# A decoder layer on one core: softmax sums on four column groups, their inverse copied to the other rows, values projected in the banks of q and k

## The reference, cut to what matters

```python
q = einsum('bse,hed->bhsd', x, Wq) + bq          # k and v alike
scores = einsum('bhsd,bhtd->bhst', q, k) / sqrt(64)
attn = softmax(where(causal, scores, -inf))
out = einsum('bhst,bhtd->bhsd', attn, v)
x = layernorm(x + out @ Wo + bo)
x = layernorm(x + cross_attention(x, ctx))
x = layernorm(x + fp8_ffn(x))
```

## Time and profile before

| what | us |
|---|---|
| median of 3 runs | 430.06 (429.84 to 430.45) |
| the profiled execution, whole | 428.27 |
| its span, from the first to the last instruction | 426.5 |
| PE busy | 385.7 |
| DVE busy | 307.5 |
| ACT busy | 237.6 |
| POOL busy | 239.8 |

### The profile page before, as it was taken

One profiled execution on the slowest core, in us unless ns is written; L12 is line 12 of the kernel. 1 busy time (PEld: TensorE's weight loads), 2 busy tenths in 40 slices (PEclk: granted clock), 3 DMA queues, 4 the chain that ended last, 5 costly groups with the idle time before them and its releaser, 6 DMA issues.

```text
span 426.5 us, 9900 instructions
## 1 busy us (share of the span) xinstructions
PE 385.7 (90%) x3698; PEld 274.1 (64%) x3698; DVE 307.5 (72%) x924; ACT 237.6 (56%) x352; POOL 239.8 (56%) x338
## 2 busy tenths in 40 slices
PE   3779999999999999999999999799999999998821
PEld 1567666776767776677766767577787776544410
DVE  0646887877887777887788877976535655689897
ACT  2335665556665566665666556464512155788941
POOL 3466876556665565655667556465824430231775
PEclk9989999999999999999999999999999999999985
DMA  8012011000000300000000000000000000000001
GB/s 259 12 6 54 3 15 27 4 8 5 5 1 5 100 2 2 3 4 1 2 3 2 2 2 3 0 2 2 3 1 2 2 0 2 2 2 2 25 26 51
DMA packets 41568, 6.96 MB, mean 16 GB/s; under 512 B 38320, under 2 KB 40240, under 8 KB 41392
## 3 DMA queue, kind: packets, MB, share of 16 engines
q1 hardware_dynamic: 41520, 6.32, 9.3%
HBM read 5.12 MB, written 1.05 MB: 14 GB/s over the span
## 4 chain that ended last, share of the span: by engine, by line
PE 64%; DVE 14%; ACT 7%; DMA 7%; issue 4%; SPq 3%; POOLq 0%; POOL 0%; DVEq 0%; ACTq 0%
PE banks L172 11%; PE banks L146 10%; PE banks L214 8%; PE banks L699 7%; DMA shift<-neg_max 6%; PE banks L152 4%; PE banks L191 4%; DVE unused L352 3%; PE banks L130 3%; PE banks L743 3%; PE banks L165 3%; SPq L523 3%; PE banks L756 3%; ACT q_hi L305 2%; PE banks L163 2%
## 5 line engine op out<-in xcount | busy, mean ns | idle before, releaser
L286 ACT ACTIVATE probs<-banks 128x768 f32<-128x768 f32 (+1 forms) x96 | 84.9, 884 | 114.1 <-PE banks L152 114.1
L352 DVE CUSTOM_DVE_ANT_0 unused<-banks,neg_mask 128x512 bf16<-128x512 f32 (+3 forms) x256 | 112.6, 487 | 38.8 <-PE banks L130 38.8
L451 POOL TENSOR_SCALAR_AFFINE_SELECT probs<-probs 128x256 f32<-128x256 f32 x128 | 51.2, 412 | 112.7 <-ACT probs L286 111.3
L172 PE MATMUL banks<-probs,v_nat 128*64 128x256 f32 (+3 forms) x512 | 74.4, 433 | 0.0
L172 PEld LDWEIGHTS banks<-probs,v_nat 128*64 128x64 f32 x512 | 36.6, 137 | 45.3 <-issue 40.5
L152 PE MATMUL banks<-shift,ones_r 64*128 64x256 f32 (+3 forms) x256 | 42.9, 329 | 6.7 <-DMA shift<-neg_max 6.6
L898 POOL TENSOR_TENSOR rstd<-var_e,halves 128x4 f32<-128x4 f32 (+1 forms) x16 | 14.4, 898 | 60.1 <-DVE var_e L974 59.8
L146 PE MATMUL banks<-q_hi,k_hi 64*128 64x256 f32 (+3 forms) x256 | 43.5, 334 | 1.7 <-ACT probs L286 1.7
L361 DVE SCALAR_TENSOR_TENSOR q_lo<-banks,bias_qk,q_hi 128x512 fp32r<-128x512 f32 x32 | 24.0, 751 | 25.8 <-ACT q_hi L305 25.8
L146 PE MATMUL banks<-q_hi,k_lo 64*128 64x256 f32 (+3 forms) x256 | 41.9, 321 | 0.0
L146 PE MATMUL banks<-q_lo,k_hi 64*128 64x256 f32 (+3 forms) x256 | 41.8, 320 | 0.0
(11 more groups left out here) (125 smaller groups left out, 826.1 us busy)
## 6 DMA issues: line engine op xcount, KB each, us to landing
shift<-neg_max SPq DMA_DIRECT2D x256, 0.5 KB, 2.0
attn_t<-w_qkv SPq DMA_DIRECT2D x1, 1344.0 KB, 7.0
attn_t<-xT SPq DMA_DIRECT2D x4, 256.0 KB, 7.2
x_s<-x_nat SPq DMA_DIRECT2D x1, 1024.0 KB, 5.1
wo_s<-wo SPq DMA_DIRECT2D x1, 512.0 KB, 3.9
out<-y_out SPq DMA_DIRECT2D x2, 256.0 KB, 3.1
out<-y_out SPq DMA_DIRECT2D x4, 128.0 KB, 1.7
neg_mask<-causal SPq DMA_DIRECT2D x1, 256.0 KB, 3.8
```

The costliest lines, as they stand in the source:

```text
L172: last = mm(o_ps[HALF[h], j * T:S], v_nat[:, v // 2 % 2, j, v % 2, HALF[h]], p_of(v, j, h, 0, S - j * T), start=(j == 0), stop=(j == NT - 1))
L286: nc.scalar.activation(probs[:, v % 2, AT[j]:AT[j] + 2 * n].rearrange("p (h s) -> p h s", h=2), st[:, :, 0:n], ACT.Exp, scale=D ** -0.5).t ...
L352: last = V.tensor_tensor_reduce(out=unused[:, h, at:at + n], in0=mx[:, h, at:at + n], in1=neg_mask[:, S - n:S], scale=-1.0, scalar=3.0e38, ...
L451: return nc.gpsimd.affine_select(out=blk, in_=blk, compare_op=ALU.is_ge, fill=0.0, base=0, pattern=pattern + [[1, T]], channel_multiplier=-1)
```

## The change

`sums` uses four column groups of 32 rows, one product each for two parts of the columns of either head. The first 32 rows of a head's 64 hold the sums of columns 0 to 255, the second 32 rows those of columns 256 to 511; the other half of every row is filled with 1.0 once, at the start. After `inverse`, the missing halves of `r_neg` are copied from one group of rows to the other: `spread` on ScalarE copies two pieces of 32 rows by 256 columns for head 0, and `inverse` on VectorE two for head 1. `normalise` waits for both, and stands one slot later, between the maxima and `q_lo`. Since bank 7 must keep its 1.0, `values` moves to banks 4 and 5, where q and k are projected; both halves of it stand together at the start of a slot, for unit u instead of u + 1, and `project` of the same slot waits for their copy. The lists of the rest of the layer are put in another order.

```diff
+        def missing(h, half):
+            cols = slice(half * S // 2, (half + 1) * S // 2)
+            return r_neg[PART[h][1 - half], cols], r_neg[PART[h][half], cols]
...
             def sums(v):
                 pe.wait_ge(added, 4 * v + 4)
-                if has(v + 2):
-                    pe.wait_ge(v_out, v + 3)
-                elif v:
-                    pe.wait_ge(o_out, v)
+                if v:
+                    pe.wait_ge(neg_out, v)
                 for h in (0, 1):
-                    mm(su[HALF[h], 0:T], ones64[:, :], p_of(v, 0, h, 0, T), start=True, stop=True)
+                    mm(su[PART[h][0], 0:T], ones32[:, :], p_of(v, 0, h, 0, T), start=True, stop=True)
+                    mm(su[PART[h][1], S // 2:], ones32[:, :], p_sum[:, v % 2, h, T:3 * T], start=True, stop=True)
                 for h in (0, 1):
-                    last = mm(su[HALF[h], T:S], ones64[:, :], p_sum[:, v % 2, h, :], start=True, stop=True)
+                    last = mm(su[PART[h][0], T:2 * T], ones32[:, :], p_sum[:, v % 2, h, 0:T], start=True, stop=True)
                 last.then_inc(sum_done, 1)
...
             def weigh(v):
                 pe.wait_ge(masked, 3 * v + 3)
+                pe.wait_ge(v_out, v // 2 * 2 + 2)
+                if v:
+                    pe.wait_ge(o_out, v)
...
             def values(v, part):
                 if part == 0:
-                    if v >= 3:
-                        pe.wait_ge(o_out, v - 2)
+                    if v < LAST:
+                        pe.wait_ge(ql_out, v + 2)
+                        pe.wait_ge(kl_out, v + 2)
+                    else:
+                        pe.wait_ge(v_out, LAST)
...
-                        last = mm(banks[:, 6 + at, 0:4 * D], x[HALF[h], tile:tile + T],
+                        last = mm(aux[at][:, 0:4 * D], x[HALF[h], tile:tile + T],
...
             def project(v, part):
-                    if v:
-                        pe.wait_ge(ql_out, v)
-                        pe.wait_ge(kl_out, v)
+                    if v == 1:
+                        pe.wait_ge(ql_out, 1)
+                        pe.wait_ge(kl_out, 1)
+                    elif v:
+                        pe.wait_ge(v_out, v - 1)
...
@@ TensorE, slot @@
                 if has(u):
+                    values(u, 0)
+                    values(u, 1)
                     scores(u, 0)
...
-                    bias()
-                    context_keys()
-                if has(u + 1):
-                    values(u + 1, 0)
+                    values(LAST, 0)
+                    values(LAST, 1)
...
-                if has(u + 1):
-                    values(u + 1, 1)
                 if has(u + 2) and u > -2:
                     project(u + 2, 1)
+                if u == LAST - 1:
+                    bias()
+                    context_keys()
...
@@ ScalarE, slot @@
+                if has(u - 2):
+                    spread(u - 2)
                 if has(u):
+                    values(u)
                     exponentials(u, 0)
...
+            def spread(v):
+                act.wait_ge(neg_out, v + 1)
+                for half in (0, 1):
+                    last = nc.scalar.copy(*missing(0, half))
+                last.then_inc(wide_out, 1)
...
@@ VectorE, slot @@
                 if has(u + 1):
                     maxima(u + 1, 0)
                     maxima(u + 1, 1)
+                if has(u - 2):
+                    normalise(u - 2)
...
                 if has(u - 1):
                     inverse(u - 1)
-                    normalise(u - 1)
...
+                dve.wait_ge(neg_out, v + 1)
+                for h, half in ((1, 0), (1, 1)):
+                    last = V.tensor_copy(*missing(h, half))
+                last.then_inc(own_out, 1)
...
             def normalise(v):
-                dve.wait_ge(neg_out, v + 1)
+                dve.wait_ge(wide_out, v + 1)
+                dve.wait_ge(own_out, v + 1)
...
+            V.memset(su[:, :], 1.0)
...
-    "n0": "y0 t0 q0 y2 y3 o00 p10 t3 q3 u1 z1 o20 u2 z2b o30 f3b",
+    "n0": "y0 t0 q0 y2 y3 q2 u0 t3 z0 p11 o11 z1 p21 f0 z2a x1 p31 u3 x3a",
...
-            scores(31, 0); y(0, 0); sums(30); y(0, 1); scores(31, 1); y(0, 2); context(); y(0, 3); weigh(30)
+            scores(31, 0); sums(30); y(0, 0); context(); y(0, 1); scores(31, 1); y(0, 2); scores(31, 2); y(0, 3)
```

## The result

The changed kernel takes 446.25 us (median of four), the one before 430.23: ratio 1.0358, 95% interval 1.0315 to 1.0402. The four include one launch of 1259.53 us, for which no trace shows a cause; the ratio leaves it out, and the other three lie at 444.31 to 447.19 with 445.3 in the middle. The prediction was 433.3, in a range up to 438.

What follows compares the result with a forecast made beforehand. TensorE bound the kernel, VectorE close behind; the change would add a wait for v_out. 28 slots at +0.17 us gave +4.7, ends -1.3, first slots -0.2: +3.2, profiled 431.5, median 433.3 us, range 427.5 to 438.

Steps and rivals of the forecast that it cites:

- Both halves of the values take 2 x 0.35 ... project could start at m + 7.0.: TensorE's list, from m, the second maxima's start: values' halves 0.35 us each, so TensorE alone could reach project at m + 7.0.
- the second limit of the prediction: VectorE's reading of the first maxima: second maxima no sooner than 1.97 us behind the first, slot 8.68 by this alone.
- Its own chain, over the copies: neg_out, ScalarE's r_neg copies, values' copy, first exponential, then scores group 1: next m at m + 8.87, taken as 8.9.
- The new order there I can't price from rows: 0, with -2 to +2 as bounds: Last 80 us of the layer, where VectorE and ScalarE lead: the rearranged lists were put at 0 us.
- Together -1.3: Both ends: bank 7's fill nothing, bias product -0.7, last sums -0.86 partly lost again, new order 0; in all -1.3 us.
- the 0.2 taken off for the first slots: Slots at the start, where the new wait is not yet in: 0.2 us less, from +3.4 to +3.2.
- the bias product's cover: Last slot of self attention: the bias product covers TensorE's 0.82 us wait for an exponential, -0.7 us.
- The maxima bind: Rival: copies hidden, VectorE's maxima set the slot at 8.68, 8.86 with late DMAs; 428 us, faster; chance 0.18.
- The copies are dear: Rival: ScalarE's r_neg copies 0.51 us each without overlap, 0.32 more a slot, 439 us; chance 0.16.
- A tie: Rival: chain through the copies 0.15 us shorter, 0.30 a copy, exponential not awaited; -0.8 us, within 0.2%; chance 0.14.
- The groups don't run side by side: Rival: sums keep their 0.9 us, TensorE reaches project at m + 7.4; the forecast's time; no chance of its own.
- All of the saving arrives: Rival: TensorE stays the bound and the sums' whole 13.8 us is gained, 416.3 us; chance 0.04.

Runs made afterwards that it cites:

- e7: Kernel before, with both halves of the values side by side at the first half's place, still in banks 6 and 7: 442.88 us, 1.0282.
- e2: Changed kernel with ScalarE's two copies of r_neg behind the first exponential instead of ahead of the values' copy: 442.73 us, 1.0287.
- e8: Changed kernel with the rest of the layer in the kernel before's order, bank table and norm lists: 441.74 us, 1.0258.
- e10: e9 with the rest of the layer in the order of the kernel before, the best full version: 438.11 us, 1.0177.
- e12: e9 with the first two exponentials of a unit on half their columns, the other half of those probabilities left at 1.0: 435.01 us, 1.0128.
- e1: Changed kernel with the first half of the values inside the weighted values, ahead of their last two products: 448.1 us, 1.0396.
- e3: Changed kernel with the edits of both e1 and e2: 445.14 us, 1.0341.
- e9: Changed kernel with the first maxima between the halves of the values on TensorE, and r_neg copies behind the first exponential: 442.84 us, 1.0266.
- e5: Changed kernel with second maxima behind project's second half, normalise between VectorE's first two maxima steps, r_neg copies behind the first exponential: 450.36 us, 1.0438.
- e11: Kernel before with only the sums on four column groups, without the copies to the other rows, logarithm of a constant: 425.99 us, 0.9887.
- e4: Changed kernel with the sums again on two column groups of 64 rows, copies kept: 453.19 us, 1.0522.

## Why the prediction was wrong

**Where the error lies.** For the profiled execution +3.2 us were forecast, and its span grew by 16.1. For the 24 slots of the table it was 24 x 0.17 = 4.1, measured 8.3; for all the rest it was -0.9, measured +7.8. So 4.2 us of the error are in the slots and 8.7 at the two ends. With the slots alone off, the time would have been 437.5, just inside the range.

**The step that failed in the slot** is one line: "Both halves of the values take 2 x 0.35 ... project could start at m + 7.0." The durations were taken from rows in which other work stood between the halves, and with it the wait on `v_part`, which stands in the code, was empty. Side by side they take 1.17 us, of which 0.10 came over from group 0 of the scores; the wait is 0.37, and e7 shows the same in the old kernel (1.07 for 0.70). Another 0.11 comes from the pieces ahead of them: the sums saved 0.34 and not 0.43, and the product behind them took 0.05 more. So TensorE comes to the first maxima at m + 7.18 instead of m + 6.7, and the second limit of the prediction, 1.97 behind that, which it gave as 8.68, becomes 9.15. The prediction had the price of the maxima's wait but not the lateness that it is added to.

Its own chain, over the copies, was sized well up to its last term: group 1 of the scores starts at 209.78, m + 8.25, where m + 8.18 was forecast. But it was given 0.69 and took 0.89: 0.10 in its first product, which starts after a stop (0.28 until the next, 0.18 before), and 0.09 in the wait for VectorE at its end. That gives 9.14 as well. The two paths are level, and so e2, which takes the copies out of one of them, changes no slot.

**The steps that failed at the ends** are "The new order there I can't price from rows: 0, with -2 to +2 as bounds", which cost some 4 us (e8, e10), "Together -1.3", and the 0.2 taken off for the first slots, where 2.8 were lost.

**Right, in its size:** neg_out at m + 6.0 (207.53 - 201.53 = 6.00); the two copies 0.74 (forecast 0.70); the values' copy done at m + 7.34 (7.32); normalise hidden in VectorE's gap; the sums 0.57 (forecast 0.49); late DMAs 0.07 a slot (forecast 0.16). The chain of copies did not bind alone, except in one slot (e2): there it cost 1.1 us. Of the bias product's cover, forecast at 0.7, the slot before unit 31 shows 1.3: it fell from 10.60 to 9.26 us.

**Half seen:** the wait for the second exponential stood in the prediction at 0.17, and for the first at 0.1. Both are there. What it did not see is that they have one cause, the missing filling between the groups of scores (e12), and that this makes the slot nearly stiff: of four orders on TensorE with the values in the new banks and the sums on four groups, three lie between 9.15 and 9.21 (the changed kernel and e2; e1 and e3; e9), and e5 above.

**What the traces show of the ends.** At the start 2.8 us were lost. In the first units the values wait for q_lo and k_lo of the next unit, with nothing ahead of them in TensorE's list that could run; its timeline there (idle before in brackets):

```profile
19.43 0.58 PE L204 MATMUL banks<-w_hi,x_hi 64*128 64x256 f32 x2 [2.97 <-issue]
...
29.90 0.39 PE L204 MATMUL banks<-w_hi,x_hi 64*128 64x256 f32 x2 [2.00 <-issue]
```

VectorE's k_lo ends at 19.33 and 29.79, just ahead of the two. The kernel before stops for other things in these slots, and e7, which has not these two stops, reaches unit 4 no earlier (53.8 us; a DMA of 3.54 us stands in its chain there). How much of the 2.8 us they cost is not shown.

From unit 31 on it is +4.1. About 2.5 of it is the bias product, which moved behind the second maxima (1.98 and 0.52 us in the chain) and so from one row of the table to the other; the slot before it is 1.3 shorter. In this trace 2.3 is the new order (e8). The saving of the last sums does not show. A part may be TensorE's clock: the last piece z ran at 1.2 GHz, and the same eight products take 0.89 us earlier:

```profile
385.44 0.89 PE banks L717 x8
...
424.81 2.09 PE banks L717 x8
```

The granted clock was halved from 413 us in the kernel before and from 421 in the changed one, for the last 13 and 22 us. Ahead of it TensorE was busy for 2.83 of the 5 us from 405 on in the kernel before, and for 2.63 of the 5 us from 415 on in the changed one. What the longer stretch costs was not tried. Against a large share speaks e11: its clock is halved for the last 18 us, and the stretch from unit 31 to its end is 130.8 us, where the kernel before has 130.9.

**The rivals.** "The maxima bind" had one of the right places and the wrong sign, since it assumed that TensorE arrives early. "The copies are dear" came nearest in time with its 439, but the copies took 0.37 each and not 0.51: a hit would have been luck. "A tie" wanted cheaper copies and no wait for the exponential, and neither came. "The groups don't run side by side" is refuted by e4. "All of the saving arrives" is refuted even for the groups alone (e11).

## What to carry to other kernels

Work that stands between a producer and its consumer is doing two jobs: when it is moved out, price the turn-around that it filled (here 1.07 us from the work behind a group of scores, over the exponential, to the next group), not only its own duration. Two stretches that add into the same banks, the second of which waits for the first by a semaphore, cost nothing more apart and 0.37 us more together; look for such waits in the code before taking durations from rows where they were empty. And in a kernel whose slot has several limits within 0.3 us of each other, ask for each stretch of the list when it can start at the earliest, with the lateness of all before it, instead of comparing chains one at a time. A step priced at 0 for want of rows, as the new order was, needs a run of its own: here it cost as much as the slots' error.

## What the runs showed of the hardware

- A stretch of TensorE that waits by a semaphore for the one before it: 0.38 us from the last product's start to the next stretch's, instead of 0.12; the first product behind it takes 0.22 until the next instead of 0.12. Together about 0.37 us (e7: 1.07 for 0.70).
- A change between 64-row and 64-column tiles costs about 0.2 us: two more of them took 0.36 us (e1). The change from 32 to 64 columns is cheap: weigh 2.30 instead of 2.25 us, in e11 as in the changed kernel.
- Four column groups of 32 do run side by side with unequal lengths: 0.57 us for 256 columns a group, 0.91 for 512 on two groups.
- A copy of 32 rows by 256 columns in SBUF costs ScalarE 0.37 us in a row with another, and VectorE 0.59 us for two; its own duration on ScalarE, 0.41 us on average, is that of the cast of 128 x 256, so the few rows save nothing that shows.
